# A four-stage transformer kernel on one core: float32 logits, later splits of the first expert's weights, and splits one chunk ahead

## The chip, the cores and the metric

One core of a Trainium2 chip runs the whole program. TensorE (PE) multiplies matrices and transposes, VectorE (DVE), ScalarE (ACT) and GpSimd (POOL) work on tiles in SBUF and PSUM, SyncE (SP) and GpSimd issue transfers (DMA). The engines run side by side, each through its own instructions in order, and wait for each other by semaphores. The metric is the time of one execution on the device in microseconds (us); less is better. TensorE's clock has two levels, 2.4 GHz (granted clock 1.00) and 1.2 GHz (0.50).

## What is computed

Two attention layers and two expert layers change a tensor x of 4 x 512 rows of 256 values:

```
x = x + L0_xattn(ctx, layernorm(x))
x = x + L0_ffn(layernorm(x))
x = x + L1_xattn(ctx, layernorm(x))
x = x + L1_ffn(layernorm(x))

# L0_ffn: 8 experts, top 2, capacity 512 rows per expert
scores = softmax(xf @ w_router)
expert_weights, top_experts = top_k(scores, 2)
... rows sorted by expert, at most 512 of each ...
h = gelu(einsum('ech,ehf->ecf', xb, w1))
y = einsum('ecf,efh->ech', h, w2)
out = zeros.at[src].add(flat_w * y) + bias

# L1_ffn: 8 experts, weights of the top 2 logits, no capacity
logits = xf @ Wr + br
weights = softmax(where(logits >= second_largest, logits, -inf))
h = gelu(einsum('td,edh->eth', xf, W1) + b1)
out = einsum('etd,te->td', einsum('eth,ehd->etd', h, W2) + b2, weights)
```

## The kernel before

Four functions run in turn: `attention0`, `experts` for layer 0, `attention1`, `experts` for layer 1. Only `experts` is changed. Products that need more than float16 are made of float16 pairs: a value is split into a high part (ScalarE's copy to float16) and a low part (VectorE's subtraction of the high part).

An expert layer has an opening and a loop. The **opening**, in the order of the data:

- TensorE transposes the 2048 rows of X (line 1469, 32 transposes in 8 groups of four, over four PSUM banks `psH0..2`, `psX`). ScalarE copies each group to float16 (`xth`, line 1422), VectorE subtracts (`xtl`, `turned_low`, line 1601), and TensorE takes the next group of a bank only after that. VectorE also computes mean and variance (lines 1581, 1586), GpSimd the inverse deviation (line 1357).
- TensorE multiplies the transposed rows with the router's weights (high by high, high by low, low by high; line 1489), and ones with the weights for the column sums (line 1481). VectorE turns the products of the rows as they are into the logits of the normalized rows (lines 1643 to 1652).
- ScalarE writes the normalized rows `xn` (`normalize`, line 1414) in two halves of eight, then splits four pieces of the first expert's weights (`split_high`, line 1174), and then computes the exponential (line 1428). VectorE finds the two best experts (to line 1668), subtracts the low parts of the same four pieces (`split_low`, line 1180), and takes the rank of each row within its expert, for which TensorE multiplies triangular ones (line 1501).
- From the ranks VectorE builds one-hot tiles in the room of `xn` (lines 1703, 1707; line 1701 waits until `xn` is written to DRAM), TensorE multiplies them (line 1528), and the result is the list of rows for each chunk: `gidx` for the gathers (line 1711), `sidx` for the scatters (line 1715).
- In layer 1 TensorE also transposes the experts' weights of each row (line 1518, ScalarE copies them, line 1434) and multiplies them with the output biases b2 (`pe_weighted_bias`, line 1509, float32, eight times; ScalarE copies each to `wb`, line 1438). Four stand before the products of line 1528, four behind.

SyncE's queue has, in order: small inputs, the weights of expert 0 (`load_weights`, 1 MB for each half), the normalized rows to `xrow` as they come, their gates, the two halves of expert 1, a base copy of X to the output sums (`yd`, lines 1280, 1281), and then the halves of experts 2 to 7. A half is loaded as soon as `split_low` has used up the same half of the expert before (`s_wl`), since the stage tile holds one expert. GpSimd's queue has the gathers of chunks 0 and 1 (line 1363), four accumulating writes to `yd` once the base copy has landed (line 1386), then for each chunk the gather two chunks ahead and the scatter of its outputs (line 1369).

The **loop** runs over chunks of 256 rows, 16 in layer 0 (two for each expert) and 23 in layer 1, two chunks in each pass. In a chunk TensorE goes through eight f: a hidden product (`pe_hidden`, lines 1128 to 1130), and two f later an output product (`pe_output`, lines 1141 to 1146); at f = 3 it turns the next chunk's rows (`pe_turn`, line 1117). ScalarE applies GELU twice (lines 1197, 1199), VectorE subtracts (line 1228). While there are experts left, ScalarE and VectorE split one expert's weights in each chunk, two experts ahead (`EARLY = 2`): chunk n splits expert n + 2. `LOOPS` is a first loop with splits (chunks 0 to 5), and a second one without; the last chunks are `TAIL`.

## Time and profile before

| | us |
|---|---|
| median of 3 runs | 2648.18 |
| lowest, highest | 2645.94, 2649.96 |
| the profiled run | 2640.42 |
| its span in the trace | 2638.5 |

| engine | busy in the span |
|---|---|
| PE | 2416.2 us, 92% |
| DVE | 1898.3 us, 72% |
| ACT | 1675.3 us, 63% |
| POOL | 1727.5 us, 65% |

The profile is of one execution. Its timeline gives the start and duration of operations on each engine, and in brackets how long the engine stood idle before and what ended that wait. The four stages lie at 0 to 1474, 1475 to 1720, 1725 to 2295, and 2296 to 2638 us, roughly. The page's slices show TensorE nearly full through the attention layers and the loops, and nearly empty in two places, the openings of the expert layers, where the granted clock is low too, and where the DMA engines are busiest. A busy share says little there: what counts is which engine waits for which.

### The profile page before, as it was taken

What the parts mean: (1) busy time and instruction counts of PE and PEld (TensorE: products, weight loads), DVE (VectorE), ACT (ScalarE), POOL (GpSimd) and SP (SyncE); (2) the same over time, 40 slices, a digit from 0 to 9 for tenths busy, and PEclk for the clock granted to TensorE, in tenths of its full rate; (3) what the DMA queues carried; (4) which work ended last, traced back from release to release, by engine and by line L of the source; (5) the groups of instructions that cost most, each with busy time, mean ns of one, the idle gap of its engine ahead of it and who ended that gap; (6) DMA issues with size and microseconds to landing.
All of it is one profiled execution on the core that took longest, in us unless ns stands there. A gap on an engine that the chain in (4) does not pass through costs nothing. (4 is left out here: it accounts for less than half of the span.)

```text
span 2638.5 us, 45921 instructions
## 1 busy us (share of the span) xinstructions
PE 2416.2 (92%) x14931; PEld 1423.0 (54%) x15058; DVE 1898.3 (72%) x3499; ACT 1675.3 (63%) x2694; POOL 1727.5 (65%) x1503
## 2 busy tenths in 40 slices
PE   5999999999999999999999479959999999879997
PEld 3455555555555555555554258844444444458886
DVE  6778777787778876767777566438888889777443
ACT  4556665656665666665666366537887888768664
POOL 2677877787777778777778345416777779824543
PEclk9999999999999999999999589988999999969998
DMA  4000000000000000000000284232111110176223
GB/s 139 8 1 1 26 1 1 1 1 1 26 1 1 1 1 1 1 1 1 1 1 1 83 242 110 45 103 51 44 33 42 34 30 21 34 215 174 48 44 66
DMA packets 88424, 107.89 MB, mean 41 GB/s; under 512 B 16370, under 2 KB 77763, under 8 KB 88211
## 3 DMA queue, kind: packets, MB, share of 16 engines
q1 hardware_dynamic: 69044, 80.57, 9.9%
q0 software_dynamic: 19200, 24.97, 5.8%
q8 instruction: 107, 1.75, 0.3%
q14 instruction: 73, 0.60, 0.1%
HBM read 68.75 MB, written 25.88 MB: 36 GB/s over the span
## 5 line engine op out<-in xcount | busy, mean ns | idle before, releaser
L424 POOL TENSOR_TENSOR a_acc<-a_acc,a_pf 128x512 f32<-128x512 f32 (+1 forms) x480 | 654.8, 1364 | 310.7 <-ACT a_pf L576 289.0
L576 ACT ACTIVATE a_pf<-a_psS 128x1024 f32<-128x1024 f32 (+1 forms) x288 | 280.9, 975 | 307.3 <-PE a_psS L718 301.1
L2060 POOL TENSOR_TENSOR c_pl<-c_pf,c_ph 128x512 f16<-128x512 f32 x320 | 375.0, 1200 | 127.6 <-ACT c_ph L2159 127.2
L870 DVE TENSOR_TENSOR a_pl<-a_pf,a_ph 128x512 f16<-128x512 f32 x448 | 433.8, 978 | 24.1 <-ACT a_ph L582 23.9
L846 DVE TENSOR_REDUCE a_mx<-a_psA 128x1 f32<-128x512 f32 x501 | 334.8, 683 | 46.2 <-PE a_psA L654 41.0
L1369 POOL DMA_INDIRECT f_sums<-f_xn,f_sidx x78 | 139.9, 1793 | 225.4 <-DVE f_xn L1734 190.1
L582 ACT ACTIVATE a_ph<-a_psS 128x1024 f16<-128x1024 f32 (+1 forms) x288 | 281.0, 976 | 0.0
L2391 DVE TENSOR_REDUCE c_mx<-c_psA 128x1 f32<-128x512 f32 x384 | 246.7, 682 | 22.5 <-PE c_psA L2230 22.3
L2152 ACT ACTIVATE c_pf<-c_psS 128x1024 f32<-128x1024 f32 x192 | 197.5, 1029 | 69.3 <-PE c_psS L2264 68.1
L1228 DVE TENSOR_TENSOR f_xn<-f_xn 128x256 f16<-128x256 f32 x312 | 129.2, 423 | 122.9 <-ACT f_xn L1199 119.6
L740 PE MATMUL a_psO<-a_pl,a_vh 128*128 128x512 f16 (+1 forms) x544 | 206.8, 380 | 5.7 <-POOL a_pl L442 5.7
L734 PE MATMUL a_psO<-a_ph,a_vh 128*128 128x512 f16 (+1 forms) x544 | 207.2, 381 | 4.0 <-DVE a_ol L875 3.9
L841 DVE TENSOR_TENSOR a_vl<-a_psA,a_vh 128x256 f16<-128x256 f32 (+1 forms) x264 | 111.3, 422 | 137.3 <-ACT a_vh L510 134.7
L595 PE MATMUL a_psS<-a_qh,a_kh 128*128 128x512 f16 (+1 forms) x544 | 206.4, 379 | 2.9 <-DVE a_bb L855 2.7
L735 PE MATMUL a_psO<-a_ph,a_vl 128*128 128x512 f16 (+1 forms) x544 | 206.9, 380 | 0.0
L597 PE MATMUL a_psS<-a_qh,a_kl 128*128 128x512 f16 (+1 forms) x544 | 206.7, 380 | 0.0
L596 PE MATMUL a_psS<-a_ql,a_kh 128*128 128x512 f16 (+1 forms) x544 | 206.7, 380 | 0.0
L2159 ACT ACTIVATE c_ph<-c_psS 128x1024 f16<-128x1024 f32 x192 | 197.7, 1030 | 0.0
L654 PE MATMUL a_psA<-a_kh,a_qh 128*128 128x512 f16 x501 | 190.1, 380 | 3.8
L1128 PE MATMUL f_psH<-f_xh,f_w 128*128 128x256 f16 x624 | 172.8, 277 | 18.5 <-ACT f_xn L1199 9.5
L835 DVE SCALAR_TENSOR_TENSOR a_kl<-a_psA,a_bkv,a_kh 128x512 f16<-128x512 f32 (+1 forms) x158 | 103.7, 656 | 118.5 <-ACT a_kh L504 118.4
L1129 PE MATMUL f_psH<-f_xl,f_w 128*128 128x256 f16 x624 | 172.4, 276 | 0.0
(354 smaller groups left out, 6308.7 us busy)
## 6 DMA issues: line engine op xcount, KB each, us to landing
f_stage<-in_L_ffn_w SPq DMA_DIRECT2D x16, 1024.0 KB, 6.0
f_stage<-in_L_ffn_W SPq DMA_DIRECT2D x16, 1024.0 KB, 6.1
c_kst<-c_khs SPq DMA_DIRECT2D x64, 100.1 KB, 2.2
a_cx<-in_ctx SPq DMA_DIRECT2D x4, 1536.0 KB
c_cx<-in_ctx SPq DMA_DIRECT2D x12, 512.0 KB, 4.0
f_xrow<-f_xn SPq DMA_DIRECT2D x8, 512.0 KB, 3.0
f_sums<-X SPq DMA_DIRECT2D x2, 2048.0 KB, 12.5
c_kst<-c_kls SPq DMA_DIRECT2D x32, 100.1 KB, 2.2
```

The lines of the kernel that those rows point to most:

```text
L424: g.tensor_tensor(acc[0:k, p, :], acc[0:k, p, :], pf[0:k, q % RF, i, :], ALU.add).then_inc(s_acc, 1)
L576: act.activation(pf[0:r, q % RF, 0:k, :], psS[q % 2][0:r, 0:k, :], ACT.Exp, scale=SCALE).then_inc(s_pF, 1)
L582: act.activation(ph[0:r, q % RP, 0:k, :], psS[q % 2][0:r, 0:k, :], ACT.Exp, scale=SCALE).then_inc(s_pH, 1)
L596: pe.matmul(out, hi, xl_, start=False, stop=False)
L597: return pe.matmul(out, lo, xh_, start=False, stop=last)
L734: pe.matmul(psO[:, :], vh[0:r, g % 2, j, vs], ph[0:r, q % RP, i, :], start=(j == 0), stop=False)
L735: pe.matmul(psO[:, :], vl[0:r, g % 2, j, vs], ph[0:r, q % RP, i, :], start=False, stop=False)
L740: ins = pe.matmul(psO[:, :], vh[0:r, g % 2, j, vs], pl[0:r, q % RP, i, :], start=False, stop=(j == JT0 - 1))
L846: v.tensor_reduce(mx[:, n % 2, it, c:c + 1], ps[:, 0:KCH[c][1]], AX.X, ALU.max).then_inc(s_fr, 1)
L870: v.tensor_tensor(pl[0:r, q % RP, i, :], pf[0:r, q % RF, i, :], ph[0:r, q % RP, i, :], ALU.subtract).then_inc(s_pL, 1)
L2060: g.tensor_tensor(pl[0:r, q % RP, i, :], pf[0:r, q % RF, i, :], ph[0:r, q % RP, i, :], ALU.subtract).then_inc(s_pG, 1)
L2391: ins = v.tensor_reduce(mx[:, n % 2, it, c:c + 1], ps[:, 0:KCH[c][1]], AX.X, ALU.max)
```

## The change

- **Logits.** `xt` holds the transposed rows in float32 (in the same room), ScalarE only copies; TensorE waits for that copy (`s_tH`). The router's products and the column sums are float32 products of `xt`, `onesf` and `wr` themselves: 32 and 2 per layer in place of 96 and 4 in float16. `turned_low`, `wrh`, `wrl` and `rstdw` are gone.
- **The opening of ScalarE and VectorE.** The exponential stands between the two halves of `normalize`. All eight pieces of expert 0 are split behind that, on VectorE behind `sidx`. Expert 1's splits leave the opening. `warm` is one GELU of a column ahead of the loop.
- **Splits one ahead.** Chunk n splits expert n + 1. The splitting loop still has three passes (`SM` = 3), then the two chunks of m = 3 are written out (the first with splits), then the second loop. TensorE waits for the second half of an expert's splits before that expert's first output, and for the first half before the first hidden product.
- **Layer 1.** One weighted bias moves from behind the products of line 1528 (1533 in the new file) to between the third and the last quarter of them. The wait for the table of experts (`s_tab`) moves behind the first two hidden products.

```
-            act.wait_ge(s_small, 16 * NSMALL)
-            act.activation(wrh[:, :, :], wr[:, :, :], ACT.Copy, scale=WS).then_inc(s_wr, 1)
             for i in range(GI):
                 kk, q = i % KC, i // KC
                 act.wait_ge(s_tP, i + 1)
-                act.activation(xth[:, kk, q * 512:q * 512 + 512], ring4[i % 4][:, :], ACT.Copy).then_inc(s_tH, 1)
+                act.activation(xt[:, kk, q * 512:q * 512 + 512], ring4[i % 4][:, :], ACT.Copy).then_inc(s_tH, 1)
             normalize(0)
-            normalize(1)
-            for q in range(PH):
-                split_high(act, 0, q)
             act.wait_ge(s_sh, 1)
             act.activation(ex[:, :, :], sh[:, :, :], ACT.Exp).then_inc(s_ex, 1)
-            for q in range(PH, PIECES):
+            normalize(1)
+            for q in range(PIECES):
                 split_high(act, 0, q)
...
-            for q in range(PIECES):
-                split_high(act, 1, q)
+
+            act.wait_ge(s_const, 3)
+            act.activation(warm[:, :], onef[:, :], GELU)
             act_turn(act, main, 0, 0)
...
                 if i >= 4:
-                    pe.wait_ge(s_tL, i - 3)
+                    pe.wait_ge(s_tH, i - 3)
...
                 for kk in range(KC):
-                    for j, (a, w) in enumerate(((xth, wrh), (xth, wrl), (xtl, wrh))):
-                        ins = pe.matmul(psY[0][:, t * E:(t + 1) * E], a[:, kk, ts], w[:, kk, :],
-                                        start=(kk == 0 and j == 0), stop=(kk == KC - 1 and j == 2))
+                    ins = pe.matmul(psY[0][:, t * E:(t + 1) * E], xt[:, kk, ts], wr[:, kk, :], start=(kk == 0),
+                                    stop=(kk == KC - 1))
...
             for i in range(2 * NT):
                 q, t = i // NT, i % NT
+                if layer and i == 2 * NT - 2 * NT // NLO:
+                    pe_weighted_bias(NB2)
                 pe.wait_ge(s_hi, q + 1)
...
-            for q in range(PH):
-                split_low(v, 0, q)
             v.wait_ge(s_rk, 1)
...
-            for q in range(PH, PIECES):
+            for q in range(PIECES):
                 split_low(v, 0, q)
...
-            for q in range(PIECES):
-                split_low(v, 1, q)
...
             for f in range(2, FT):
                 pe_hidden(pe, L, n, p, e, f)
+                if f == 2 and fresh:
+                    pe.wait_ge(s_wl, (n + 2) * PIECES)
                 pe_output(pe, L, n, p, e, f - 2)
...
             if splits:
-                pe.wait_ge(s_wl, (n + 3) * PIECES)
+                pe.wait_ge(s_wl, (n + 2) * PIECES + PH)
...
                 if splits:
-                    split_high(act, n + EARLY, f)
+                    split_high(act, n + 1, f)
...
-            for first_m, last_m, splits in LOOPS:
-                with act.Fori(first_m, last_m) as m:
-                    for p in range(2):
-                        act_chunk(act, main, m, p, splits)
+            with act.Fori(0, SM) as m:
+                for p in range(2):
+                    act_chunk(act, main, m, p, True)
+            for p in range(2):
+                act_chunk(act, main, SM, p, p == 0)
+            with act.Fori(SM + 1, PAIRS) as m:
+                for p in range(2):
+                    act_chunk(act, main, m, p, False)
```

ScalarE in the opening of layer 0, before (L1414 is `normalize`, L1174 `split_high`, L1428 the exponential, L1184 the turn of chunk 0):

```order
L1422 ACTIVATE f_w<-f_psX 128x512
L1414 ACTIVATE f_xn<-X,f_shift,f_rstd 128x256 x16
L1174 ACTIVATE f_w<-f_stage 128x512 x4
L1428 ACTIVATE f_ex<-f_sh 128x128
L1174 ACTIVATE f_w<-f_stage 128x512 x12
L1184 ACTIVATE f_xh<-f_psX 128x512
```

and after (L1418, L1427, L1176, L1186 are the same four; L1442 is `warm`):

```order
L1424 ACTIVATE f_w<-f_psX 128x512
L1418 ACTIVATE f_xn<-X,f_shift,f_rstd 128x256 x8
L1427 ACTIVATE f_ex<-f_sh 128x128
L1418 ACTIVATE f_xn<-X,f_shift,f_rstd 128x256 x8
L1176 ACTIVATE f_w<-f_stage 128x512 x8
L1442 ACT_TABLE_LOAD
L1442 ACTIVATE f_warm<-f_onef 128x1
L1186 ACTIVATE f_xh<-f_psX 128x512
```

The exponential moved ahead of eight normalizations and four splits, eight splits left, and a table load came in. The table load in front of line 1197, within the loop before, is gone.

VectorE in layer 0 from the choice of experts to the ranks, before (L1668 is the selection, L1180 `split_low`, L1693 the first operation on the ranks):

```order
L1668 TENSOR_TENSOR f_sel<-f_oh 128x128
L1679 TENSOR_SCALAR f_wst<-f_sc 128x128
L1180 SCALAR_TENSOR_TENSOR f_w<-f_stage,f_w 128x512 x4
L1693 TENSOR_TENSOR f_eq<-f_psY,f_lim 128x128
L1694 SCALAR_TENSOR_TENSOR f_cand<-f_eq,f_psY 128x128
```

and after:

```order
L1659 TENSOR_TENSOR f_sel<-f_oh 128x128
L1670 TENSOR_SCALAR f_wst<-f_sc 128x128
L1682 TENSOR_TENSOR f_eq<-f_psY,f_lim 128x128
L1683 SCALAR_TENSOR_TENSOR f_cand<-f_eq,f_psY 128x128
L1684 TENSOR_TENSOR f_at<-f_oh,f_cand 128x256
```

The four splits between the selection and the ranks are gone.

TensorE at the end of the opening of layer 1, before (L1518 transposes the rows' weights, L1509 is the weighted bias, L1528 the one-hot products):

```order
L1518 MATMUL f_psH<-identf,f_wgt 8x128 x16
L1509 MATMUL f_psH<-f_b,f_wt 128x256 x8
L1528 MATMUL f_psY<-f_xn 128x46 x32
L1509 MATMUL f_psH<-f_b,f_wt 128x256 x8
L1117 MATMUL f_psX<-identf,f_xb 128x128 x4
```

and after:

```order
L1521 MATMUL f_psH<-identf,f_wgt 8x128 x16
L1512 MATMUL f_psH<-f_b,f_wt 128x256 x8
L1533 MATMUL f_psY<-f_xn 128x46 x24
L1512 MATMUL f_psH<-f_b,f_wt 128x256 x2
L1533 MATMUL f_psY<-f_xn 128x46 x8
L1512 MATMUL f_psH<-f_b,f_wt 128x256 x6
L1117 MATMUL f_psX<-identf,f_xb 128x128 x4
```

One weighted bias (two products) moved into the one-hot products.

## Rows read from the trace of the kernel before

**Rows 1.** Timeline, VectorE, layer 0: start, duration (us), engine, line, operation, count [idle before].

```profile
1490.39 0.29 DVE L1646 TENSOR_TENSOR f_eq<-f_psY,f_sc 128x128 f32<-128x128 f32 x1
...
1496.87 0.28 DVE L1660 TENSOR_REDUCE f_sm<-f_ex 128x16 f32<-128x128 f32 x1 [5.22 <-ACT f_ex L1428]
...
1501.71 2.49 DVE L1180 SCALAR_TENSOR_TENSOR f_w<-f_stage,f_w 128x512 f16<-128x512 f32 x4
1504.12 0.28 DVE L1693 TENSOR_TENSOR f_eq<-f_psY,f_lim 128x128 f32<-128x128 f32 x1
...
1516.27 0.19 DVE L1711 TENSOR_SCALAR f_gidx<-f_psY 128x32 uint32<-128x32 f32 x1 [1.29 <-PE f_psY L1528]
```

**Rows 2.** Timeline, ScalarE, opening of layer 0.

```profile
1486.60 7.96 ACT L1414 ACTIVATE f_xn<-X,f_shift,f_rstd 128x256 f32<-128x256 f32 x16
...
1496.54 0.30 ACT L1428 ACTIVATE f_ex<-f_sh 128x128 f32<-128x128 f32 x1
```

**Rows 3.** Timeline, TensorE, layer 0: transposes, ranks, first hidden product, third turn.

```profile
1474.92 2.79 PE L1469 MATMUL f_psH<-identf,X 128*128 128x128 f32 x12 [5.89 <-PEq L329]
...
1502.01 1.03 PE L1501 MATMUL f_psY<-f_sel,f_ones 128*128 128x120 f16 x15
...
1530.41 0.39 PE L1128 MATMUL f_psH<-f_xh,f_w 128*128 128x256 f16 x1 [2.95 <-DVE f_xl L1207]
...
1555.31 1.11 PE L1117 MATMUL f_psX<-identf,f_xb 128*128 128x128 f32 x4 [1.79 <-DMA f_xb<-f_xrow,f_gidx]
```

**Rows 4.** Timeline, GpSimd, layer 0: accumulating writes, first scatter.

```profile
1533.57 5.35 POOL L1386 DMA_DIRECT2D f_sums<-f_bias  x4 [10.28 <-DMA f_sums<-X]
...
1554.49 1.66 POOL L1369 DMA_INDIRECT f_sums<-f_xn,f_sidx  x1 [12.59 <-DMA f_sums<-f_bias]
```

**Rows 5.** Lines 1509 and 677: duration in ns min/median/max, starts, forms.

```profile
L1509 PEld LDWEIGHTS f_psH<-f_b,f_wt x32: 283/332/333, 2322.6 to 2340.3; 8*128 8x128 f32 x32
...
L677 PEld LDWEIGHTS a_psA<-a_brow,a_onef x2: 182/184/185, 67.9 to 68.0; 1*128 1x128 f32 x2
```

**Rows 6.** Timeline, TensorE's weight loads, line 677.

```profile
67.91 0.29 PEld L677 LDWEIGHTS a_psA<-a_brow,a_onef 1*128 1x128 f32 x2
```

**Rows 7.** Windows: busy and count of PE, PEld, DVE, ACT, POOL; PEclk, DMA, GB/s.

```profile
67.80:68.20 0.40, 0.40 (x5) 0.35 (x4) 0.40 (x2) 0.00 (x0) 0.00 (x0) 1.00 0.00 0
1486.00:1488.00 2.00, 1.44 (x53) 1.35 (x51) 1.85 (x11) 1.89 (x4) 1.14 (x2) 0.50 0.00 0
2300.00:2302.00 2.00, 1.08 (x9) 0.80 (x8) 1.85 (x8) 1.77 (x5) 1.63 (x2) 1.00 0.91 375
2302.00:2304.00 2.00, 0.36 (x4) 0.12 (x3) 1.85 (x6) 0.92 (x2) 0.29 (x1) 0.81 1.04 379
2326.00:2328.00 2.00, 2.00 (x6) 1.53 (x6) 2.00 (x11) 0.60 (x1) 0.00 (x0) 0.50 0.00 0
```

**Rows 8.** Timelines of layer 1: TensorE's start, VectorE, ScalarE, TensorE.

```profile
2296.63 2.79 PE L1469 MATMUL f_psH<-identf,X 128*128 128x128 f32 x12 [2.48 <-PEq L1917]
...
2310.57 0.29 DVE L1646 TENSOR_TENSOR f_eq<-f_psY,f_sc 128x128 f32<-128x128 f32 x1
...
2316.70 0.29 DVE L1671 TENSOR_TENSOR f_eq<-f_lg,f_m 128x128 f32<-128x128 f32 x1 [0.86 <-ACT f_ex L1428]
...
2325.74 7.22 DVE L1707 TENSOR_SCALAR f_xn<-f_ilo,f_lo,f_tid 128x128 f16<-128x128 f16 x32
...
2334.26 0.21 DVE L1711 TENSOR_SCALAR f_gidx<-f_psY 128x46 uint32<-128x46 f32 x1 [1.30 <-PE f_psY L1528]
...
2321.97 0.59 ACT L1434 ACTIVATE f_wt<-f_psH 8x512 f32<-8x512 f32 x1 [0.27 <-PE f_psH L1518]
...
2322.61 7.19 PE L1509 MATMUL f_psH<-f_b,f_wt 8*128 8x256 f32 x16 [0.68 <-ACT f_wt L1434]
...
2329.73 0.96 PE L1528 MATMUL f_psY<-f_xn 128*128 128x46 f16 x16
```

**Rows 9.** Groups of instructions by line, ScalarE: count, busy, mean ns, idle before.

```profile
L1197 ACT ACT_TABLE_LOAD x6 | 7.7, 1283 | 5.7 <-PE f_psH L1130 5.4
```

86 lines of the change are left out of this document (38 added, 48 removed).

## The prediction, made before the changed kernel ran

> **What bounds the kernel now.** The program runs four stages one after the other, and only the two expert layers (the first from 1474.9 us, the second from 2296.6 us) are touched. I read the two openings engine by engine in the timelines, then what the loop waits for at its start, then the duration and the clock of the operations that the change brings in. In the first layer VectorE has the logits' last inputs at 1490.39, works on, and then idles 5.22 us for the exponential, because ScalarE runs 16 row normalizations (7.96 us) and four weight splits first [rows 1, 2]. It splits four weight pieces (2.49 us) before the ranks, and has the gather list at 1516.27 [rows 1]. TensorE starts the expert loop at 1530.41, and its third turn of rows (line 1117) waits for a gather until 1555.31 [rows 3]. That gather stands on GpSimd's queue behind the four accumulating writes, which were issued at 1533.57, when the base copy had landed, and held GpSimd's wait until 1554.49 [rows 4]. So the openings are a chain: logits, exponential, ranks, row lists, gather, then transfers; what makes the list earlier moves everything behind it, and stages C and the end follow the loops.
>
> **Logits by float32 products.** Removed per layer: eight subtractions and two small operations on VectorE, 100 float16 products on TensorE. Added: 34 float32 products (2 column sums, 32 logits) with 128x128 stationary data, in front of the logits. The transposes no longer wait for VectorE: 32 of them run on end. At half clock 12 took 2.79 us, 0.215 each [rows 3]; at full clock I halve that. In the second layer the clock was at full rate (2.4 GHz) 3.4 us after their start, before at half (1.2 GHz) [rows 7, 8]. So the first layer's transposes end at about 1480.9 (23 at half clock, 9 at full), the second's at about 2301.7 (16 and 16). ScalarE's copies, now free of the small loads, keep up.
>
> What one float32 product costs no row shows for this shape. The trace has two records for each (line 1509: 16 in the program, 32 records), and each record loads its weights again. Two such loads of 128 columns took 0.29 us together, each 0.184 long, so they start 0.106 us apart, at clock 1.00 [rows 5 to 7]; the moving 8 columns hide under that. At clock 0.50 I double it to 0.213; the load's duration of 0.332 there fits [rows 5, 7]. 68 loads are 7.2 us at full clock and 14.5 us at half. The float16 ones went at 53 products in 2 us at half clock, and were nearly free [rows 7].
>
> Which clock? After the transposes the array moves only 8 columns per load. In the second layer the full clock came at 2300 and was going again in 2302 to 2304, and float32 products with 8 rows of data, back to back, stayed at half clock [rows 7]. I take 3 us at full clock (28 loads) and the other 40 at half (8.5 us): 11.5 us. The logits then stand at 1492.4 against 1490.39, **+2.0**, and at 2313.2 against 2310.57, **+2.6** [rows 1, 8]. VectorE itself would be ready some 4 us earlier than before and then waits. Bounds: -2.2 and -1.6 with all loads at full clock, +5.0 and +5.6 with all at half.
>
> A rule speaks against this edit. The Trainium skill, "TensorE: Matmul & The Clock Gate", section on weight-path perf modes, says that the fast weight load is on for 128 weights of any type but float32; the rows agree (0.106 us against some 0.027 at half the clock). The same page, section LDWEIGHTS, gives P/1.2 ns for P columns whatever the clock; by it 68 loads would be 7.3 us (an estimate from that page) and the sum the one of the second rival below.
>
> **Exponential ahead, splits behind the lists, first layer.** From the logits on: the wait of 5.22 us shrinks to the exponential's own 0.30 and two hand-overs, say 0.48: -4.74. The four splits leave (line 1693 starts 2.41 us after them) [rows 1], but they covered the rank products (1.03 us [rows 3], with hand-overs some 1.4 us from the selection), which VectorE now waits for: -1.0. The second half of the normalizations now runs behind the exponential: 4 us, and some 3.5 until the last row write lands, about 8 us after the exponential's input. VectorE needs that at line 1701 some 9 us after it: hidden, with 1 us to spare (the row writes' 3.5 us are an estimate from the page's median of 3.0 to landing). Together **-5.75**; if that cover is gone, -4.
>
> **The same in the second layer.** VectorE gains 0.86 (its wait for the exponential) and the four splits, 3.3 us [rows 1, 8]. But the lists need TensorE too. Before, ScalarE copied the last weight transposes (line 1434) at 2321.97, the four weighted biases (float32, half clock) started at 2322.61 and ended 7.1 us later, when the one-hot products start, 2329.73; VectorE's one-hots began at 2325.74, so TensorE was already late and caught up in the last quarter [rows 8]. Now ScalarE has four more normalization-lengths and eight splits (4 + 4.25 us) between exponential and line 1434. Counted from the end of the logits' shift (2312.16 before: five operations of 0.3 from 2310.57 on): last copy ends at 11.5, biases end at 18.7, 24 one-hot products 19.9, the fifth weighted bias (1.7) 21.6, last eight and the list 22.8. Before it was 22.1 (list at 2334.26) [rows 8]. VectorE alone would have allowed 18.9. So its gain is lost here and the list comes **+0.7** later. The ends are -3.2 (TensorE's float32 products at full clock) and +2.
>
> **From the list to the third turn.** Weights are now split one expert ahead, so both loads of expert 1 (1 MB each) are issued after the list, then the base copy, and the loads of expert 2 wait for chunk 0; before, four loads fell between list and chunk 0's middle. ScalarE is no longer held by a load before its first turn, VectorE has only 8 splits there: chunk 0 starts about 1.4 us sooner after the list (before 14.1 us). ScalarE's first split in chunk 1, which waited for a load before, stays late, since its load is now issued in chunk 0 and meets the accumulating writes. The base copy lands at the same distance from the list: 1 MB more stands ahead of it, 2 MB of later loads no longer beside it. The writes have one load less beside them, 1 MB of some 5 in 20.6 us [rows 4]. The third turn comes **-2.4** per layer against the list, -4.8 in all; between 0 (base copy later by the megabyte ahead of it, 2.4 us) and -8 (no half-clock stretch behind a shorter stall).
>
> **The loops.** The table load (1.283 us, six in the trace, three per layer, one for each pass of the splitting loop [rows 9]) is done once before the loop by the `warm` activation, under the wait for the gather. ScalarE has slack in most passes, so I count some 0.3 for each pass: -1.8 in all. A seventh chunk with splits and one more entry into a loop cost some +0.65 per layer. Net **-0.5**. The waits added in TensorE's chunk (first expert output at f = 2, first hidden product of the next chunk) stand behind splits that VectorE did before the values those products need anyway; nothing.
>
> **Sum.** +4.6 - 5.75 + 0.7 - 4.8 - 0.5 = -5.75 us. On the profiled span of 2638.5 (its run 2640.42, and 7.8 us under the median) that is 2632.75; on the median of 2648.18 it is **2642.4**.
>
> **Rivals.** *The clock stays full.* If weight loads count as work for the clock, all 68 go at 0.106: logits -3.8 instead of +4.6, sum -14.2, 2634.0. For it: the loads are back to back behind dense transposes. Against: the float32 stretch of the second layer at 0.50 [rows 7]. The Trainium skill's figure of the section LDWEIGHTS gives this case too.
> *The clock is never granted, or falls at once*: +10.6, sum +0.25, 2648.4. The first layer's opening showed 0.50 even after its transposes [rows 7].
> *Slower: loads don't overlap.* If a float32 record of this small shape holds the array for its whole recorded load, 0.332 us at half clock [rows 5], 68 are 22.6 us: logits +26.9, sum +16.6, 2664.8. It makes the kernel slower by over 0.2% from about 0.25 us per record. Against it: two loads started 0.106 us apart.
> *The transfers take it back.* If the base copy lands later by the extra megabyte (2.4 us in each layer), the list's lead shrinks before the third turn: sum -0.95, 2647.2. A list that is earlier is still kept, so this can't make it slower by itself.
> That the edit is idle is no case: the order above shows the exponential and the splits moved.
>
> **How the numbers follow.** Forecast 0.50, full clock 0.15, half clock 0.15, transfers 0.12, no overlap 0.08. A measurement tells about 0.2% (5.3 us) from no change. The forecast lies just beyond that, so 0.6 of its chance counts as faster (0.30), with the full clock 0.45, and 0.05 more from mixtures: 0.50; slower 0.09; the rest, 0.41, the same. The range must take in full clock with a little more behind the list and half clock or transfers with 3 us of scatter: 2633 to 2652, which leaves out the rival without overlap and half a tenth at each end.
>
> **What would show it.** Right: float32 loads of the logits 0.107 us apart, then 0.213; logits at +2 in both layers; first layer's wait for the exponential under 0.6 us and its list about 3.7 us earlier; second layer's list some 3 us later, TensorE (not VectorE) last there; six table loads down to two; third turn 36 to 37 us after the list (before 39). Wrong: the clock at 1.00 through the logits, a wait of VectorE for the row writes before the one-hots, or a base copy that lands over 18 us behind the list.

## The result, and the profile after

The changed kernel is slower: 2654.26 us (median of 14 runs, 2650.65 to 2660.35) against 2648.02 of the kernel before in the same comparison (14 runs), a ratio of 1.0026 with a 95% interval from 1.0018 to 1.0033. That is +6.2 us where -5.75 was forecast, and it lies above the range (2633 to 2652). (A difference of two medians and a difference worked out from the ratio can lie some 0.7 us apart; below, a difference against the kernel before is worked out from the ratio, except that of a single execution.) The profiled execution took 2653.72 us with a span of 2651.9 us, 13.4 us more than the span before; about 7 us of those belong to the profile of before, which lay that much under its median.

The lists did come as hoped. Timeline of VectorE, layer 0, after: start, duration, line, operation, idle before.

```profile
1491.61 0.29 DVE L1637 TENSOR_TENSOR f_eq<-f_psY,f_sc 128x128 f32<-128x128 f32 x1 [3.90 <-PE f_psY L1492]
...
1493.31 0.29 DVE L1651 TENSOR_REDUCE f_sm<-f_ex 128x16 f32<-128x128 f32 x1 [0.43 <-ACT f_ex L1427]
...
1499.52 0.29 DVE L1682 TENSOR_TENSOR f_eq<-f_psY,f_lim 128x128 f32<-128x128 f32 x1 [1.28 <-PE f_psY L1504]
...
1511.70 0.19 DVE L1700 TENSOR_SCALAR f_gidx<-f_psY 128x32 uint32<-128x32 f32 x1 [1.32 <-PE f_psY L1533]
```

The wait for the exponential is 0.43 us instead of 5.22 [rows 1], the four splits are gone from in front of the ranks, and VectorE waits 1.28 us for the rank products instead. The stage's first transpose starts at 1476.44 (1474.92 before [rows 3]), so the list stands 35.26 us after it, 6.1 us sooner than the 41.35 before. What follows the list gives it back. Timelines of SyncE's queue, of GpSimd and of TensorE, layer 0, after:

```profile
1514.88 2.78 SPq L1265 DMA_DIRECT2D f_stage<-in_L_ffn_w  x2
1517.70 0.58 SPq L1283 DMA_DIRECT2D f_sums<-X  x1
```

```profile
1531.12 5.35 POOL L1390 DMA_DIRECT2D f_sums<-f_bias  x4 [12.39 <-DMA f_sums<-X]
1536.77 1.10 POOL L1367 DMA_INDIRECT f_xb<-f_xrow,f_gidx  x1 [0.30 <-issue]
...
1551.97 1.63 POOL L1373 DMA_INDIRECT f_sums<-f_xn,f_sidx  x1 [12.65 <-DMA f_sums<-f_bias]
```

```profile
1520.10 1.12 PE L1117 MATMUL f_psX<-identf,f_xb 128*128 128x128 f32 x4 [8.44 <-DMA f_xb<-f_xrow,f_gidx]
...
1553.51 1.11 PE L1117 MATMUL f_psX<-identf,f_xb 128*128 128x128 f32 x4 [8.80 <-DMA f_xb<-f_xrow,f_gidx]
```

Counted from the list (1511.70), the base copy `f_sums<-X` is issued at +6.0, the accumulating writes (line 1390) at +19.4, the first scatter, which waits for them, at +40.3, and the third turn starts at +41.8. Before, the same points were +3.6, +17.3, +38.2 and +39.0 [rows 1, 3, 4]. The base copy on SyncE's queue before:

```profile
1519.85 0.58 SPq L1280 DMA_DIRECT2D f_sums<-X  x1
```

TensorE has its first rows sooner (turn 0 at +8.4, before +10.1) and runs through two chunks quickly, only to wait 8.80 us for the third chunk's rows, where it had waited 1.79 us [rows 3]. In layer 1 the third turn went from +37.2 to +42.5.

### The profile page after: what moved, and what is told of

Same layout as the page of the kernel before. It is cut to its first block and busy times, and to the rows that moved or that the text cites. A ratio compares the mean times of both kernels' runs of the same rounds, so it can differ in the third digit from the quotient of the medians.

```text
span 2651.9 us, 45640 instructions
## 1 busy us (share of the span) xinstructions
PE 2428.5 (92%) x14867; PEld 1435.3 (54%) x14994; DVE 1892.5 (71%) x3479; ACT 1670.3 (63%) x2690; POOL 1726.9 (65%) x1505
## 5 line engine op out<-in xcount | busy, mean ns | idle before, releaser
L870 DVE TENSOR_TENSOR a_pl<-a_pf,a_ph 128x512 f16<-128x512 f32 x448 | 436.4, 984 | 23.4 <-ACT a_ph L582 23.3
L846 DVE TENSOR_REDUCE a_mx<-a_psA 128x1 f32<-128x512 f32 x501 | 334.7, 684 | 45.5 <-PE a_psA L654 40.8
L2382 DVE TENSOR_REDUCE c_mx<-c_psA 128x1 f32<-128x512 f32 x384 | 246.9, 683 | 22.5 <-PE c_psA L2221 22.3
L1128 PE MATMUL f_psH<-f_xh,f_w 128*128 128x256 f16 x624 | 173.5, 278 | 23.7 <-ACT f_xn L1201 11.2
L1130 PE MATMUL f_psH<-f_xh,f_w 128*128 128x256 f16 x624 | 173.0, 277 | 0.0
```

The lines of the kernel that those rows point to most:

```text
L846: v.tensor_reduce(mx[:, n % 2, it, c:c + 1], ps[:, 0:KCH[c][1]], AX.X, ALU.max).then_inc(s_fr, 1)
L870: v.tensor_tensor(pl[0:r, q % RP, i, :], pf[0:r, q % RF, i, :], ph[0:r, q % RP, i, :], ALU.subtract).then_inc(s_pL, 1)
L2382: ins = v.tensor_reduce(mx[:, n % 2, it, c:c + 1], ps[:, 0:KCH[c][1]], AX.X, ALU.max)
```

## The experiments

All times of a kernel are set against the kernel before on the same chip, since the chips differ: before had medians of 2647.9, 2643.8, 2648.5 and 2647.4 us in the four sets. Kernels of different sets are compared by their ratios. before_again (set 2), before_same_chip (set 3) and a_hold_loads (set 4) were executed once, for their profiles.

| kernel | set | median us | ratio to before [95%] |
|---|---|---|---|
| after | - | 2654.3 | 1.0026 [1.0018, 1.0033] |
| after_again (unchanged) | 3 | 2658.3 | 1.0036 [1.0024, 1.0048] |
| p1_logits | 1 | 2645.0 | 0.9991 [0.9982, 1.0000] |
| p2_exp_splits | 1 | 2648.4 | 1.0001 [0.9992, 1.0010] |
| p3_one_ahead | 1 | 2651.4 | 1.0012 [1.0003, 1.0021] |
| p12_no_one_ahead | 4 | 2650.7 | 1.0013 [1.0004, 1.0022] |
| b_base_first | 2 | 2639.5 | 0.9982 [0.9973, 0.9991] |
| p3_base_first | 3 | 2634.5 | 0.9946 [0.9933, 0.9958] |
| a_base_first | 1 | 2628.0 | 0.9924 [0.9910, 0.9938] |
| a_gather_first | 2 | 2645.7 | 1.0006 [0.9997, 1.0015] |
| a_base_first_wt | 2 | 2622.3 | 0.9917 [0.9904, 0.9931] |
| c_f16 | 3 | 2619.9 | 0.9891 [0.9877, 0.9906] |

The points of the chain in each profile, in us: logits and list from the layer's first transpose; base copy issued, writes issued, first scatter and third turn from the list; then the time from the third to the last turn. Each pair is layer 0 / layer 1.

| kernel | logits | list | base | writes | scatter | third turn | third to last |
|---|---|---|---|---|---|---|---|
| before | 15.5 / 13.9 | 41.4 / 37.6 | 3.6 / 3.6 | 17.3 / 17.3 | 38.2 / 36.4 | 39.0 / 37.2 | 150.4 / 232.5 |
| after | 15.2 / 15.5 | 35.3 / 39.5 | 6.0 / 6.1 | 19.4 / 20.4 | 40.3 / 41.3 | 41.8 / 42.5 | 152.0 / 237.2 |
| before_again | 15.3 / 14.0 | 41.1 / 37.7 | 3.6 / 3.6 | 16.9 / 17.2 | 38.1 / 37.1 | 38.9 / 38.0 | 151.5 / 232.9 |
| before_same_chip | 16.1 / 14.0 | 42.0 / 37.7 | 3.6 / 3.7 | 16.9 / 17.5 | 39.0 / 36.4 | 39.9 / 37.8 | 152.4 / 235.1 |
| after_again | 15.2 / 15.6 | 35.3 / 38.9 | 6.0 / 6.1 | 19.4 / 19.6 | 43.2 / 43.8 | 43.7 / 44.3 | 151.5 / 236.9 |
| p1_logits | 16.6 / 16.0 | 37.8 / 38.7 | 3.6 / 3.7 | 17.1 / 17.3 | 38.3 / 36.6 | 39.1 / 37.4 | 152.3 / 234.7 |
| p2_exp_splits | 16.0 / 14.0 | 36.1 / 38.1 | 6.0 / 6.1 | 20.0 / 19.7 | 39.9 / 39.9 | 40.8 / 40.8 | 152.7 / 235.8 |
| p3_one_ahead | 15.9 / 13.9 | 41.8 / 37.7 | 3.6 / 3.7 | 16.8 / 17.4 | 38.1 / 37.5 | 39.0 / 38.3 | 151.5 / 236.9 |
| p12_no_one_ahead | 15.2 / 15.9 | 35.3 / 40.0 | 6.0 / 6.1 | 20.0 / 19.8 | 39.9 / 38.4 | 40.8 / 39.6 | 151.1 / 234.7 |
| a_hold_loads | 15.3 / 15.7 | 35.3 / 39.0 | 6.0 / 6.1 | 19.5 / 20.0 | 34.2 / 35.8 | 42.1 / 43.5 | 151.5 / 236.5 |
| a_gather_first | 18.4 / 15.7 | 38.4 / 39.0 | 6.0 / 6.1 | 20.4 / 20.7 | 41.9 / 39.6 | 29.4 / 33.2 | 161.6 / 237.8 |
| b_base_first | 15.1 / 14.0 | 40.9 / 37.7 | -14.1 / -14.3 | 7.0 / 6.6 | 35.7 / 37.5 | 36.8 / 38.6 | 148.6 / 231.7 |
| p3_base_first | 15.3 / 14.2 | 41.2 / 38.1 | -14.1 / -14.3 | 6.5 / 6.6 | 30.4 / 31.1 | 31.5 / 32.7 | 151.9 / 234.7 |
| a_base_first | 15.2 / 15.7 | 35.2 / 39.0 | -10.9 / -12.2 | 7.0 / 7.1 | 27.8 / 27.5 | 30.8 / 30.6 | 149.6 / 235.4 |
| a_base_first_wt | 18.4 / 15.9 | 38.4 / 36.3 | -11.0 / -9.2 | 7.0 / 7.1 | 27.5 / 27.5 | 30.7 / 30.2 | 148.4 / 232.1 |
| c_f16 | 15.3 / 13.9 | 35.3 / 34.2 | -11.0 / -9.2 | 6.5 / 7.1 | 27.7 / 26.8 | 30.2 / 29.5 | 150.0 / 235.4 |

The theory with which I went in: the base copy stands on SyncE's queue behind expert 1's second load, and that load waits for VectorE's splits of expert 0. Those now come after the list, eight instead of four, so base copy, writes and third turn are bound to the list with 2.4 us more between. Rivals: the float32 logits cost more than the openings show, or the loads do.

### Each part alone

**p1_logits.** The kernel before, with this part of the change (and what belongs to it) only:

```diff
-                    for j, (a, w) in enumerate(((xth, wrh), (xth, wrl), (xtl, wrh))):
-                        ins = pe.matmul(psY[0][:, t * E:(t + 1) * E], a[:, kk, ts], w[:, kk, :],
+                    ins = pe.matmul(psY[0][:, t * E:(t + 1) * E], xt[:, kk, ts], wr[:, kk, :], start=(kk == 0),
...
```

> The kernel before with the float32 logits alone. From the two traces the logits themselves moved -0.3 us in the first layer and +1.5 us in the second. Theory A (the base copy's place decides the third turn; this part only shifts the lists, and everything behind moves with them): +1 us, third turn 39 us after the list in layer one and 37 us in layer two, as before. Rival B (the 68 float32 loads per layer cost more than the traces' openings show, for instance through the clock in what follows): +4 us or more.

It is 2.4 us faster (0.9991, an interval that ends at 1.0000), so both theories missed the time; the third turns stand at 39.1 and 37.4 us, where theory A had them. The logits are no sooner, but the first list is, by 3.6 us. ScalarE's timeline shows why:

```profile
1481.20 4.04 ACT L1415 ACTIVATE f_xn<-X,f_shift,f_rstd 128x256 f32<-128x256 f32 x8
1485.78 4.04 ACT L1415 ACTIVATE f_xn<-X,f_shift,f_rstd 128x256 f32<-128x256 f32 x8 [0.54 <-DVEq L1592]
1489.72 2.17 ACT L1174 ACTIVATE f_w<-f_stage 128x512 f16<-128x512 f32 x4
1493.13 0.31 ACT L1427 ACTIVATE f_ex<-f_sh 128x128 f32<-128x128 f32 x1 [1.24 <-DVEq L1634]
```

Its copies of the transposes no longer take turns with VectorE's subtractions, so the normalizations begin at 1481.20 instead of 1486.60 [rows 2], and normalizations and splits are through before the exponential's input is there. The 5.22 us that VectorE waited are thus removed by this part too, and can be had only once.

**p2_exp_splits.** The kernel before with the second part only. Shown is the cut on ScalarE and VectorE; one weighted bias of layer 1 also moves on TensorE, as in the change:

```diff
             normalize(0)
-            normalize(1)
-            for q in range(PH):
-                split_high(act, 0, q)
             act.wait_ge(s_sh, 1)
             act.activation(ex[:, :, :], sh[:, :, :], ACT.Exp).then_inc(s_ex, 1)
-            for q in range(PH, PIECES):
+            normalize(1)
+            for q in range(PIECES):
                 split_high(act, 0, q)
...
-            for q in range(PH):
-                split_low(v, 0, q)
             v.wait_ge(s_rk, 1)
```

> The kernel before with the exponential ahead and all eight splits of expert 0 behind the lists, weights still split two experts ahead. Theory A: the first layer's list comes about 5.8 us sooner, but the base copy stands on SyncE's queue behind expert 1's second load, which waits for splits that VectorE now makes after the list, eight instead of four: base copy 6.0 us after the list instead of 3.6, third turn about 41.5 us after it instead of 39.0; second layer's list 0 to +1 us, its third turn +2.4 against the list. In all -1 us (between -3 and +2). Rival C (nothing is given back here, the loss is all in the third part): third turns stay 39 and 37 us behind the lists, in all -5 us.

Measured +0.3 us (0.9992 to 1.0010): in the range of the theory, and the rival's -5 is excluded. The base copy is issued 6.00 and 6.06 us after the lists instead of 3.6, the writes at 20.0 and 19.7 instead of 17.3, the third turn at 40.8 in both layers. The first list is 5.3 us sooner than before; 1.7 of that are lost again behind it, and in the second layer, where the list gains nothing, the third turn is 2.8 to 3.5 us later against it than in the profiles of before.

**p3_one_ahead.** The kernel before with weights split one chunk ahead, on all engines:

```diff
-                    split_high(act, n + EARLY, f)
+                    split_high(act, n + 1, f)
...
-            for q in range(PIECES):
-                split_high(act, 1, q)
+            act.wait_ge(s_const, 3)
+            act.activation(warm[:, :], onef[:, :], GELU)
```

> The kernel before with weights split one chunk ahead, the early table load and the rewritten loops alone. Theory A: lists stay; base copy stays 3.6 us behind them; third turn at 39 and 37 us, chunk 0 starts 1.5 to 3 us sooner after the list; the loss is in the loops (pitches of the splitting chunks): +4 to +6 us. Rival C: the loads of expert 1, now beside base copy and accumulating writes, also push the third turn back by 2 us or more per layer, +8 us in all. Rival D (my prediction): -2 us or less per layer, -5 us in all.

+3.2 us (0.8 to 5.6), against the prediction's -5, rival C's +8 and, just under it, theory A's +4 to +6. Chunk 1's rows are turned 18.2 us after the list instead of 21 to 22, but the third turn is at 39.0 and 38.3 as before: where a gather that stands behind the writes is what ends last, an earlier start of chunk 1 is a longer wait. Where the 3.2 us lie stays open: theory A had put them in the loops, but beside those of p1_logits and p2_exp_splits, on the same chip, this kernel's loop is about 1 us shorter in layer 0 and 1 to 2 us longer in layer 1.

**p12_no_one_ahead.** The first two parts together.

> Parts one and two together, without part three. Alone they gave -2.4 and +0.3 us, part three +3.2, all three +6.9 (+1.1 is the sum of the three). Theory G (one and two both remove the same wait for the exponential in the first layer): list there -5.5 to -6.1 us instead of -3.6 and -5.3 added up, second layer's list +1.5; third turns +1.7 and +3 against the lists from the base copy's later issue; in all 0 to +1.5 us against before. Then part three costs 5 to 7 us on top of them and not 3.2, since with the base copy later its loads stand beside the writes. Rival (gains add up): -2 us or less.

The lists moved as expected of the overlap: -6.1 us in layer 0, not the 8.9 of the sum (3.6 and 5.3), and +2.4 in layer 1. The time is +3.4 us (1.1 to 5.8), more than the 0 to 1.5 expected; the gains do not add up, and the rival's -2 is excluded. The third part on top of these two costs 0.0013 to 0.0023 of the time, 3.4 to 6 us, by the two comparisons of the whole change (on other chips). Between the parts' sum of +1.1 us and the whole change's +6.2 to +9.5, the 2.8 us of overlap are shown; of the rest I know only what follows on the writes.

### Where the base copy stands

**a_base_first.** The kernel after with only this moved:

```diff
+            sp.dma_start(yd[0:T, :].rearrange("(t p) c -> p t c", p=P), X[:, :, :]).then_inc(s_base, 16)
+            sp.dma_start(yd[T:T + CH, :].rearrange("(t p) c -> p t c", p=P), X[:, 0:IT, :]).then_inc(s_base, 16)
             for half in range(2):
                 load_weights(1, half)
-            sp.dma_start(yd[0:T, :].rearrange("(t p) c -> p t c", p=P), X[:, :, :]).then_inc(s_base, 16)
-            sp.dma_start(yd[T:T + CH, :].rearrange("(t p) c -> p t c", p=P), X[:, 0:IT, :]).then_inc(s_base, 16)
```

> The kernel after with the two base copies issued ahead of expert 1's two loads instead of behind them, nothing else changed. They then go out while the ranks are made, some 16 us sooner in layer one. Theory A: base copy lands before the list; the accumulating writes are issued right behind the first four gathers (first layer some 7 us after the list instead of 19.4), third turn at 31 to 33 us behind the list instead of 41.8 and 42.5: -8 to -11 us per layer, -18 us in all against the kernel after, about -12 us against the kernel before. Rival B (the third turn waits for chunk 0's and 1's own work, the clock or the loads): within 3 us of the kernel after.

-20 us against before (0.9924), some 27 us against the kernel after: more than the 18 expected, and the largest effect of all. SyncE's queue, then GpSimd, then ScalarE in layer 0:

```profile
1500.92 0.93 SPq L1280 DMA_DIRECT2D f_sums<-X  x1
1501.89 2.40 SPq L1281 DMA_DIRECT2D f_sums<-X  x1
1515.03 41.73 SPq L1265 DMA_DIRECT2D f_stage<-in_L_ffn_w  x7
```

```profile
1518.89 5.38 POOL L1390 DMA_DIRECT2D f_sums<-f_bias  x4
1524.58 1.10 POOL L1367 DMA_INDIRECT f_xb<-f_xrow,f_gidx  x1 [0.30 <-issue]
...
1539.70 1.63 POOL L1373 DMA_INDIRECT f_sums<-f_xn,f_sidx  x1 [12.27 <-DVE f_xn L1721]
```

```profile
1540.48 0.63 ACT L1176 ACTIVATE f_w<-f_stage 128x512 f32 x1 [3.71 <-DMA f_stage<-in_L_ffn_w]
```

The base copy goes out while the ranks are made, in a stretch in which the transfers were all but idle (this is the window of the kernel after; the last two columns are the share of the DMA engines and GB/s):

```profile
1505.00:1510.00 5.00, 3.31 (x24) 2.49 (x24) 5.00 (x24) 0.00 (x0) 0.00 (x0) 0.50 0.00 0
```

GpSimd has no wait for it any more (line 1390 has no bracket), the writes are issued 7 us after the list, and the first scatter waits for chunk 0's own rows (line 1721), not for the writes. The third turn comes at 30.8 and 30.6 us. What still holds chunk 1 is ScalarE's wait of 3.71 us for a load. This settles the main cause: the third turn was bound to the base copy's place. It was bound to it in the kernel before as well, since against that kernel too the third turns come 8.2 and 6.6 us sooner behind the list; so the 27 us are not all damage done by the change.

**b_base_first.** The same edit in the kernel before.

> The kernel before with its base copies issued ahead of expert 1's loads, nothing else changed. Theory A: third turn no longer bound by the writes, but chunk 1 starts only 22 us behind the list there (ScalarE and VectorE split expert 1 first), so the third turn comes at about 35 us instead of 39.0 and 37.2: -6 us in all. The kernel after with the same edit gave -20 us, so behind this edit the change is worth some -12 us, although it costs +6.9 us without it. Rival: the change itself costs its 6 us wherever the base copy stands; then this kernel runs some 6 us below a_base_first, at -26 us.

-4.7 us, so behind this edit the change is worth 0.0058 of the time, 15 us (the two intervals lie 0.0035 apart), where without it it costs 6 to 9. The mechanism I gave was half right. The third turn is still at 36.8 and 38.6, but for another reason. Timelines of GpSimd and ScalarE, layer 0:

```profile
1552.65 1.63 POOL L1369 DMA_INDIRECT f_sums<-f_xn,f_sidx  x1 [19.40 <-DVE f_xn L1734]
```

```profile
1526.20 2.19 ACT L1174 ACTIVATE f_w<-f_stage 128x512 f16<-128x512 f32 x4 [8.18 <-DMA f_stage<-in_L_ffn_w]
...
1543.84 0.63 ACT L1174 ACTIVATE f_w<-f_stage 128x512 f32 x1 [5.54 <-DMA f_stage<-in_L_ffn_w]
```

Here the first scatter waits for chunk 0's rows. ScalarE must split all of expert 1 before its first turn and expert 2 in chunk 0, and waits for their loads, which now run beside the writes. With two experts ahead the loads become the bound as soon as the base copy isn't.

**p3_base_first.** The third part with the same edit.

> Part three alone (weights one chunk ahead, early table load) with the base copies ahead of expert 1's loads. Without the base copies moved, part three cost 3.2 us; the edit of the base copies alone gave -4.7 us on the kernel before, and the writes took 28.7 and 31.0 us there, beside four loads, against 20.8 with two. Theory A (part three's fewer loads are worth something only where the writes start early): writes again 20 to 22 us, third turn 31 us behind the list, -15 to -18 us against before, so that this part alone brings most of the difference of b_base_first and a_base_first. Rival (the two other parts bring it, through the earlier list): -6 us or less.

-14.3 us (0.9933 to 0.9958), just short of the 15 to 18 expected and far from the rival's 6: the part that alone costs 3.2 us is worth 9.5 us more than b_base_first once the base copy is out of the way. The expectation reads 28.7 and 31.0 us as the writes' duration in b_base_first; that was a misreading, since the first scatter waits for VectorE there, and in this kernel and a_base_first too. The DMA's landing times put the end of b_base_first's writes 24.4 and 21.3 us behind their issue; for this kernel the trace has no landing of them, so that part of the expectation can't be judged.

**a_gather_first.** The kernel after with chunk 2's gather ahead of the writes:

```diff
+            g.wait_ge(main.xP, 3)
+            g.wait_ge(s_gate, 1)
+            gather(2)
             g.wait_ge(s_base, 32)
...
-                if n + 2 < NC:
+                if n and n + 2 < NC:
```

> The kernel after with chunk 2's gather issued ahead of the accumulating writes on GpSimd's queue (right behind the first turn, whose buffer it needs) instead of behind them; base copy and writes stay where they are. Theory A (it is the gather's place in the queue behind the writes): third turn 31 to 33 us behind the list instead of 41.8 and 42.5; chunk 3's gather still stands behind the first scatter, which waits for the writes (40 us), so the fourth turn waits some 3 us; in all -7 us per layer, -14 us against the kernel after. Rival E (it is the DMA traffic of base copy, loads and writes itself that keeps rows or weights away): third turn still 38 us or more, within 4 us of the kernel after.

The third turn is at 29.4 and 33.2 us: it was indeed the place in GpSimd's queue that held it, and not rows or weights slowed by traffic. But the ratio is 1.0006, about 5 us below the change's and not 14. TensorE's timeline shows the fourth turn:

```profile
1566.99 1.12 PE L1117 MATMUL f_psX<-identf,f_xb 128*128 128x128 f32 x4 [5.02 <-DMA f_xb<-f_xrow,f_gidx]
```

It comes 23.4 us after the third (17.8 in layer 1), since chunk 3's gather stands behind the first scatter, and that waits for the writes until 41.9 us. A queue entry moved ahead of a late one leaves the next behind it. I had put this wait at 3 us.

### What lengthens the writes

**before_again**, and then **after_again** and **before_same_chip**, both on one chip: the kernels unchanged, for further profiles.

> The kernel before, unchanged, for a second profile. The profile of before was 7.8 us under the median of its runs, the profile of after at its median. Theory S (the profile of before shows a lucky loop): lists and third turns as before within 0.5 us, but third to last turn 2 to 4 us longer in the second layer (234.5 to 236.5 instead of 232.5), as in the three kernels with one part each, whose loops have 234.7 to 236.9. Rival: 232.5 +- 0.5 again, so that every edit lengthened the loops by 2 to 4 us.

Its second layer's loop is 232.9 us, so the 232.5 of the first profile was no accident of one execution; the loops of the kernels with one part each (234.7 to 236.9) were measured on another chip.

> The kernel after, unchanged, for a profile on the same chip as one of before. The chips differ: before has 2647.9 us in the first set of experiments, 2643.8 us in the second, and the second's loops show 11.66 us at the pass boundaries where the first's show 11.8 to 12.0. Theory A: with the chip the same, third turns +1.7 to +2.8 us behind the lists in layer one and +4 to +5 in layer two, list -6 and +2, and the loops from the third to the last turn +0 to +2 us per layer instead of the +1.6 and +4.8 of the first two profiles; ratio 1.0015 to 1.003. Rival: +4.8 us in the second layer's loop again; then the loops are a cost of their own.

> The kernel before, for a profile on this chip, to be set against after_again: start of the second layer, lists, third turns and loop lengths. Expected: list 41.2 and 37.7 us after the layer's start, third turn 39.0 and 37.2 to 38.0 behind it.

On one chip the second layer's loop is 236.9 us against 235.1 and the first's 151.5 against 152.4: +0.9 us together, not the +6.4 of the first two profiles. Most of that was the chips: at the loop's pass boundaries one turn follows the other in 11.65 to 11.67 us, late in the second layer, in the second set and in the first profile of before, and in 11.8 to 12.1 in the other three sets and in the first profile of after, whichever kernel it is. What is left is the opening: lists -6.7 and +1.2 us, third turns against them +3.8 and +6.5, loops +0.9; the sum is +5.7 us, the two spans differ by 6.5 (2648.02 and 2654.55). The third turns are later than the base copy's 2.4 us explain. GpSimd in layer 1, before and then after:

```profile
2357.23 5.35 POOL L1386 DMA_DIRECT2D f_sums<-f_w  x4 [10.96 <-DMA f_sums<-X]
...
2376.16 1.63 POOL L1369 DMA_INDIRECT f_sums<-f_xn,f_sidx  x1 [10.81 <-DMA f_sums<-f_w]
```

```profile
2357.81 5.35 POOL L1390 DMA_DIRECT2D f_sums<-f_w  x4 [12.51 <-DMA f_sums<-X]
...
2382.00 1.62 POOL L1373 DMA_INDIRECT f_sums<-f_xn,f_sidx  x1 [15.45 <-DMA f_sums<-f_w]
```

From the writes' issue to the scatter it is 18.9 us before and 24.2 after. In that stretch SyncE issues two 1 MB loads before (25.6 and 31.9 us behind the list) and three after (19.8, 25.9 and 31.7): chunk 1 starts 4.6 us sooner, frees the stage buffer sooner, and calls the next load into the writes.

**a_hold_loads.** The kernel after with the later loads held until the writes are done:

```diff
+            sp.wait_ge(s_bst, 16 * NQ)
             with sp.Fori(2, E) as e:
                 for half in range(2):
                     load_weights(e, half)
```

> The kernel after with SyncE waiting for the end of the accumulating writes before it issues the loads of expert 2 and later ones. It measures what the loads cost the writes; as a version it is meant to be slow. In after three 1 MB loads are issued between the writes' issue and the first scatter (19.7, 25.2 and 31.3 us behind the list), which stands 20.9 to 24.2 us behind the writes' issue; in before two or three, 18.9 to 22.2. Theory F (a load beside the writes lengthens them by about 3 us): 17 to 18.5 us from writes to scatter in both layers, third turn's gather lands 3 us sooner, but chunk 1's splits now wait for their loads and the kernel is slower, 5 to 15 us above after. Rival (the writes have their own pace, and the differences are chance): 20.5 us or more.

GpSimd and ScalarE in layer 0:

```profile
1531.09 5.35 POOL L1391 DMA_DIRECT2D f_sums<-f_bias  x4 [12.45 <-DMA f_sums<-X]
...
1545.83 1.63 POOL L1374 DMA_INDIRECT f_sums<-f_xn,f_sidx  x1 [6.54 <-DMA f_sums<-f_bias]
```

```profile
1551.38 0.63 ACT L1176 ACTIVATE f_w<-f_stage 128x512 f32 x1 [15.41 <-DMA f_stage<-in_L_ffn_w]
```

Alone the four writes take 14.7 and 15.8 us, less than the 17 to 18.5 expected, against 18.9 to 22.2 in the profiles of before (two loads issued beside them, in before_same_chip's layer 0 a third near their end) and 20.9 to 24.2 in those of after (three, the first of which went out 0.5 to 1.2 us ahead of the writes in the first profile). So the loads lengthen the writes, by some 2 to 3 us each. This is a rough mean: in before, two earlier loads were still landing when the writes began, and they are not counted. The time did not grow by 5 to 15 us: one run is 6.4 us above its chip's before, like the change itself. The third turn stayed at 42.1 and 43.5, because chunk 1 now waits 15.41 us for the load that its splits need. In this one execution both ways end at about the same place: whoever goes first, writes or loads, makes the other late. That fits with what was measured above: the gather's earlier place brought 5 us against the kernel after, and the base copy's, which uses idle transfer time, some 27.

### Versions that beat both kernels

**a_base_first_wt.** a_base_first with ScalarE's order mended in layer 1, and TensorE's fifth weighted bias back behind the one-hot products:

```diff
-            for q in range(PIECES):
+            for q in range(0 if layer else PIECES):
                 split_high(act, 0, q)
...
                                    ACT.Copy).then_inc(s_wbF, 1)
+                    for q in range(2 * i, min(2 * i + 2, PIECES)):
+                        split_high(act, 0, q)
...
-                if layer and i == 2 * NT - 2 * NT // NLO:
-                    pe_weighted_bias(NB2)
```

> a_base_first with the second layer's order mended: ScalarE copies the transposed weights (line 1434 of after) right behind the exponential and the normalizations and makes the eight splits between the copies of the weighted biases; TensorE's fifth weighted bias stands behind the one-hot products again. If TensorE's float32 chain is what ends last before the second list (VectorE waited 5.0 us for it at line 1700), the list comes at 34.5 to 36 us from the layer's start instead of 39.0: -3 to -4.5 us against a_base_first. If VectorE's own one-hots bind: list at 38 or more, within 1 us.

VectorE in layer 1, a_base_first and then this kernel:

```profile
2324.84 0.21 DVE L1700 TENSOR_SCALAR f_gidx<-f_psY 128x46 uint32<-128x46 f32 x1 [4.22 <-PE f_psY L1533]
```

```profile
2323.86 0.21 DVE L1700 TENSOR_SCALAR f_gidx<-f_psY 128x46 uint32<-128x46 f32 x1 [1.29 <-PE f_psY L1533]
```

The wait falls to the 1.29 us that the last products need, and the list stands 36.3 us after the layer's start instead of 39.0: 2.7 us, a little short of the 3 to 4.5 expected. As a time the gain can't be told: 0.9917 on this chip, 0.9924 for a_base_first on another.

**c_f16.** The same with the logits by float16 pairs (the first part of the change undone).

> a_base_first_wt with the logits by float16 pairs, as before the change (parts two and three kept). The float32 logits stood at 18.4 and 15.9 us of their layers on the second chip, the float16 ones at 15.3 and 14.0. Theory: both lists come sooner by that, 3 and 2 us, -5 us against a_base_first_wt: ratio 0.990 (0.989 to 0.991) against before. Rival (float16's copies hold ScalarE, VectorE's subtractions come on top, and what stands behind takes it back): within 1.5 us of a_base_first_wt.

0.9891, 28.9 us under before, is the lowest ratio here, in an interval that overlaps that of a_base_first_wt; its lists stand at 35.3 and 34.2 us. The layer-1 logits are 2.1 us sooner (13.9 against 15.9). In layer 0 the float32 logits came at 18.4 us in both profiles of set 2's chip and at 15.2 to 16.6 in all others, against 15.3 here. Whether the whole 0.0026 between the two kernels is the logits' stays open, since they ran on different chips.

## Why the prediction was wrong, step by step

- **Logits by float32 products** (+2.0 and +2.6): -0.3 and +1.5 us in the profile. The mechanism and the price held: the loads start 0.112 us apart at full clock and 0.213 at half (taken as 0.106 and 0.213), which the text had named as a sign of being right. Over-sized was the share at half clock: 44 and 48 of the 68 loads ran at full clock, not 28. In the first layer the clock was also up 2.6 us after the first transpose, so the transposes ended 1.1 us sooner than worked out. This swings from one execution to another: in a_gather_first 26 of 68 ran at full clock, and the first layer's logits came at 18.4 us, where the forecast was 17.5. (The text calls the case in which all loads go at the full-clock price the second rival; it is the first one listed.) The part's real gain, that ScalarE gets through its work sooner, was not in the sum because the next term had already booked it.
- **Exponential ahead, first layer** (-5.75 from logits to list): from 25.9 to 20.1 us, -5.8. Right, with the wait of 0.43 and the 1.28 for the ranks.
- **The same in the second layer** (+0.7): +0.4 us. Right: the last copy of line 1434 ended 11.5 us after the logits' shift, the biases at 18.7, as worked out, the list came at 22.5 (22.8 worked out), and VectorE waited 5.01 us for TensorE. a_base_first_wt shows that this chain cost 2.7 us.
- **From the list to the third turn** (-2.4 per layer, bounds 0 to -8): +2.8 and +5.3, on one chip +3.8 and +6.5. This is the step that failed, by 13 us in the profiles. It said that "the base copy lands at the same distance from the list". The copy is issued behind a load that waits for VectorE's splits of expert 0; the same change had put four more of them, 2.4 us, between list and load. I had moved the splits in the sum for VectorE and not followed who waits for them on SyncE's queue. It also said that "the writes have one load less beside them" (in 20.6 us, which are 20.9 in rows 4); in the second layer they had one more (three instead of two, in the two profiles of one chip), since a faster chunk 0 and 1 call the loads sooner. That chunk 0 starts sooner was right (10.9 us after the list instead of 14.1, 3.2 us where 1.4 were expected) and brought nothing at the third turn.
- **The loops** (-0.5): +0.9 on one chip. The table loads fell from six to two [rows 9], and nothing came of it that can be measured.

The sum of the terms as they were measured on one chip is +5.7 us. The rival that transfers take the lead back came nearest in its mechanism, but it was bounded at "can't make it slower", because it counted only the megabyte ahead of the copy and kept the list's lead; the second layer has no such lead. The range was too narrow for the same reason: the bound of 0 at the third turn had no row behind it. The sign that the text named for being wrong did appear: the base copy landed just before the writes were issued, 19.4 and 20.4 us behind the list, where a landing later than 18 was to count against it.

## What to carry to other kernels

When work is moved behind a point, follow each semaphore that it raises to the other engines' queues: here splits that cost VectorE nothing held a load on SyncE, the load held a copy, and the copy held writes, gather and third turn, so a gain of 6 us became a loss. A transfer whose data is ready early belongs in front of everything that waits, in the stretch where the queues are idle; that one exchange of two queue entries made the same change worth 15 us. And two edits that remove the same wait are worth it once, while an edit that starts work sooner is worth nothing, or less, as long as something else ends last.

## What the runs showed of the hardware that I had not expected

Float32 products with 8 moving columns, back to back behind dense transposes, kept the full clock for about 5 us in the kernel after and for 3 us in the first layer of a_gather_first. Windows of layer 0, after and then a_gather_first (busy and count of PE and its weight loads first, then the granted clock):

```profile
1484.00:1486.00 2.00, 2.00 (x20) 2.00 (x20) 0.57 (x8) 2.00 (x6) 1.20 (x2) 1.00 0.88 294
1488.00:1490.00 2.00, 2.00 (x11) 2.00 (x10) 0.00 (x0) 0.00 (x0) 0.00 (x0) 0.50 0.51 173
```

```profile
1484.00:1486.00 2.00, 2.00 (x15) 2.00 (x15) 0.00 (x0) 2.00 (x5) 1.88 (x2) 0.71 0.41 140
1490.00:1492.00 2.00, 2.00 (x11) 2.00 (x11) 0.00 (x0) 0.00 (x0) 0.00 (x0) 0.50 0.00 0
```

The array is busy throughout, yet the clock falls from 2.4 to 1.2 GHz. The weight loads in the first layer of after, in the windows 1482:1486 and 1487:1491 (start, duration of the whole row, count):

```profile
1481.92 4.21 PEld L1492 LDWEIGHTS f_psY<-f_wr,f_w 128*128 128x128 f32 x37
1486.80 4.39 PEld L1492 LDWEIGHTS f_psY<-f_wr,f_w 128*128 128x128 f32 x20
```

With one load lasting 0.19 us at full clock and 0.33 at half, they start 0.112 and 0.213 us apart. The logits' 64 records (two for each of the 32 products) took 9.78 us in after and 11.60 in a_gather_first. The Trainium skill, "TensorE: Matmul & The Clock Gate", section LDWEIGHTS, gives P/1.2 ns for P columns, 0.107 us for 128. The trace agrees with that at full clock, as the distance from one load to the next (0.112 us), and not at half clock (0.213 us).

Four accumulating writes of 0.5 MB each took 14.7 and 15.8 us with no load beside them (one execution, two layers), and each 1 MB load issued beside them went with some 2 to 3 us more. From the base copy's issue to the writes, which wait for its landing, it was 13.2 to 14.7 us in all kernels whose copy was issued behind the list; the change made no such difference there.
